# A graph network on one core: the last five layers multiply by whole float32 features and widened counts

## The reference, cut to what matters

```python
for l in range(5):
    agg = segment_sum(h[src], dst, 6250)
    x = (h + agg) @ W1[l] + b1[l]
    x = relu(bn(x, bn1_g[l], bn1_b[l]))
    x = x @ W2[l] + b2[l]
    x = relu(bn(x, bn2_g[l], bn2_b[l]))
    h = relu(bn(x, bn3_g[l], bn3_b[l]))
```

## Time and profile before

| | us |
|---|---|
| median of the timed runs | 11149.94 |
| lowest and highest timed run | 11141.5, 11180.91 |
| span of the profiled execution | 11182.9 |
| TensorE matmuls busy in the span | 6422.3 (57%) |
| VectorE, ScalarE, GpSimd busy | 4061.9, 3980.1, 4429.3 |

### The profile page before, as it was taken

How to read it: one execution, slowest core, us unless ns; L and a number is a source line. 1 busy time by engine, 2 the same in 40 slices (tenths; PEclk the granted TensorE clock), 3 DMA queues, 4 the chain that set the end, 5 groups by cost and what they waited for, 6 DMA issues and landing times. The chain is left out here.

```text
span 11182.9 us, 142834 instructions
## 1 busy us (share of the span) xinstructions
PE 6422.3 (57%) x34150; PEld 4429.5 (40%) x34151; DVE 4061.9 (36%) x11422; ACT 3980.1 (36%) x8307; POOL 4429.3 (40%) x4465
## 2 busy tenths in 40 slices
PE   1611112642367787355554555545554989898997
PEld 1600001630012575255553555535554444444443
DVE  3800001442278787444444444534445020201112
ACT  2046662002278775344443444434444010101001
POOL 3866667247710000366664666466664000000000
PEclk8555555765578898677776777777777999999998
DMA  4332223534433442133332333233332546464554
GB/s 122 95 88 86 87 85 111 144 104 121 123 120 117 142 133 88 45 72 72 72 71 64 71 72 72 58 76 71 71 72 49 181 146 200 141 202 140 167 173 134
DMA packets 1106637, 1190.87 MB, mean 106 GB/s; under 512 B 118423, under 2 KB 991526, under 8 KB 1105944
## 3 DMA queue, kind: packets, MB, share of 16 engines
q1 hardware_dynamic: 710164, 628.94, 19.0%
q0 software_dynamic: 150784, 336.22, 12.6%
q10 hardware_dynamic: 245444, 222.71, 7.1%
HBM read 973.07 MB, written 216.86 MB: 106 GB/s over the span
## 5 line engine op out<-in xcount | busy, mean ns | idle before, releaser
L1196 POOL DMA_INDIRECT ring<-gat_rows,src_idx x2496 | 2426.2, 972 | 1550.8 <-issue 946.1
L1316 PE MATMUL ps<-ring,xT_b 128*128 x8192 | 1494.4, 339 | 1697.0 <-ACT xT_b L1402 1091.5
L1316 PEld LDWEIGHTS ps<-ring,xT_b 128*128 128x128 f32 x8192 | 1312.4, 243 | 1884.8 <-issue 1883.4
L1394 ACT ACTIVATE xT_a<-xT_a,state 128x514 f32<-128x514 f32 x1024 | 742.6, 725 | 2370.7 <-DVE xT_a L1364 1751.7
L1364 DVE CUSTOM_DVE_ANT_0 xT_a<-ps,mask,xT_a 128x512 f32<-128x512 f32 x1024 | 768.9, 751 | 2241.7 <-remote 1361.7
L1622 PE MATMUL ps<-xT_b,features 128*128 128x504 f16 (+1 forms) x5655 | 1198.3, 367 | 0.0
L690 POOL DMA_INDIRECT by_src<-ring,state x832 | 806.7, 970 | 462.1 <-issue 462.1
L1307 PE MATMUL ps<-ident,s_col 128*128 128x128 f32 x4096 | 750.3, 316 | 214.0 <-issue 129.9
L1622 PE MATMUL ps<-adj_tile,features 128*128 128x504 f16 (+1 forms) x3900 | 827.4, 367 | 0.0
L1046 POOL TENSOR_TENSOR x_nodes<-x_nodes,state 128x1280 f32<-128x1280 f32 x12 | 39.4, 3311 | 1971.2 <-DMA ring<-gathered 1254.2
L1817 POOL TENSOR_TENSOR features<-xT_a,features 128x640 bf16<-128x640 f32 x40 | 56.1, 1402 | 1919.7 <-DVE features L1814 1919.7
(11 more groups left out here) (379 smaller groups left out, 8639.2 us busy)
## 6 DMA issues: line engine op xcount, KB each, us to landing
dl_all<-dloc_rows ACTq DMA_DIRECT2D x1052, 128.0 KB
xT_b<-adjacency SPq DMA_DIRECT2D x145, 882.0 KB, 4.8
xT_b<-adjacency SPq DMA_DIRECT2D x145, 756.0 KB, 4.6
adj_tile<-adjacency SPq DMA_DIRECT2D x100, 882.0 KB
adjacency<-xT_b ACTq DMA_DIRECT2D x319, 252.0 KB
adj_tile<-adjacency SPq DMA_DIRECT2D x100, 756.0 KB
ring<-by_src SPq DMA_DIRECT2D x52, 1040.0 KB
ring<-gathered SPq DMA_DIRECT2D x208, 260.0 KB
```

Of the source, the lines that this page charges most:

```text
L1196: pool.indirect_dma_start(ring[:, o:o + RC], None, table[:, :], bass.IndirectOffsetOnAxis(src_idx[:, t * W + u:t * W + u + 1], 0)).then_in ...
L1316: m = pe.matmul(bank(BO + v % 2, R), pw[v % 4][:, w * P:(w + 1) * P], ring[:, w * RC:][:, bass.ds(look(SLOT, u - 7), R)], start=w == 0, st ...
L1394: act.activation(um[u % 4], sm[u % 8], ACT.Identity, bias=S[:, ER:][:, bass.ds(look(BC, u), 1)]).then_inc(q["act_a"], 1)
```

## The change

It is in four parts.

1. The features stay whole float32 (`H`, 128 columns a block), and so do the sums of the extra runs (`V`), `run_hit` and the extra counts (`extra_of`, laid out anew). There is one matmul a window in place of three, with float32 on both sides. The split is gone: `feature_to_node` and a load of the first two tiles (`preload`) take its place between layers, three copies (ScalarE, VectorE, GpSimd) and the same load before the first layer.
2. Since the counts are multiplied in float32, `widen(n)` makes a float32 copy of each 16-bit tile: VectorE the first 4 windows and ScalarE the other 3 (in part two 3 and 3, the last one narrow), into one of two buffers. TensorE waits for both halves (`eq`, `eq2`) instead of for the load; the two engines wait for the load, and for TensorE to be through with the tile two before. SyncE reloads a tile's buffer when it has been widened.
3. The taking out of part one and its bias and statistics stand inside the loop over part two, in the order of the engines' programs between the widenings.
4. The count matrix lies in DRAM in rows of 6552 counts (`adj`: 49 x 128 x 6552). A tile's load is one run of 7056 bytes a partition instead of seven of 1008. ScalarE's loop over the 319 pairs is written out; a pair that straddles two source blocks is stored with two DMAs (24 such). To make room the buffers of the earlier stages are given back before, with one more copy (`kept_extra`) and one more barrier.

```diff
-        adj = dram("adjacency", (2 * PAIRS, P, WD), F16)
+        adj = dram("adjacency", (NB, P, NWIN * WD), F16)
...
+            def widen(n):
+                k, i = divmod(n, NB)
+                b, f = n % NT, n % 2
+                for eng in (dve, act):
+                    if n >= KEPT:
+                        eng.wait_ge(q[f"ld{b}"], 16 * (n // NT + (b >= KEPT)))
+                    if n >= 2:
+                        eng.wait_ge(q["product"], n - 1)
+                cut, end = cuts[k]
+                dve.tensor_copy(wide[f][0][:, 0:cut], tiles[b][:, 0:cut]).then_inc(q["eq"], 1)
+                act.activation(wide[f][1][:, 0:end - cut], tiles[b][:, cut:end], ACT.Copy).then_inc(q["eq2"], 1)
...
             for k, ws in enumerate(parts):
                 for i in range(NB):
                     b = n % NT
                     if n >= NT:
-                        sp.wait_ge(q["product"], n - NT + 1)
+                        sp.wait_ge(q["eq"], n - NT + 1)
+                        sp.wait_ge(q["eq2"], n - NT + 1)
                     if n >= KEPT:
                         load_tile(i, ws, b)
-                        pe.wait_ge(q[f"ld{b}"], 16 * (n // NT + (b >= KEPT)))
-                    for x in range(3):
-                        h = H3[:, (i * 3 + x) * D:(i * 3 + x + 1) * D]
...
+                    if n == NB + 1:
+                        evict(parts[0])
+                    widen(n)
+                    if n == 1:
+                        dve.wait_ge(q["bcast"], 1)
+                        s(dve, lambda: dve.tensor_copy(V[0:NV, :], of_runs))
+                    if k and i % 5 == 1 and (i - 2) // 5 - 2 in parts[0]:
+                        bias_and_stats((i - 2) // 5 - 2)
+                    pe.wait_ge(q["eq"], n + 1)
+                    pe.wait_ge(q["eq2"], n + 1)
+                    h = H[:, i * D:(i + 1) * D]
+                    for j, w in enumerate(ws):
+                        v = wide[n % 2][0][:, j * WD:j * WD + width] if o < 0 else wide[n % 2][1][:, o:o + width]
+                        m = pe.matmul(bank(w % 8, width), h, v, start=i == 0, stop=False)
+                        if lo < hi:
+                            pe.matmul(bank(w % 8)[:, lo - w * WD:hi - w * WD], h, ident[:, lo - i * P:hi - i * P],
+                                      start=False, stop=False)
...
+        cuts = [(4 * WD, 7 * WD), (3 * WD, 5 * WD + width_of(NWIN - 1))]
+        wide = [(nsb(f"wide{f}", 4 * WD), nsb(f"wide{f + 2}", 3 * WD)) for f in range(2)]
...
-            sp.dma_start(tiles[b][:, 0:len(ws) * WD].rearrange("p (w c) -> p w c", c=WD),
-                         adj[i * NWIN + ws[0]:i * NWIN + ws[-1] + 1, :, :].rearrange("w p c -> p w c")
-                         ).then_inc(q[f"ld{b}"], 16)
+            n = cuts[ws[0] // DW][1]
+            sp.dma_start(tiles[b][:, 0:n], adj[i, :, ws[0] * WD:ws[0] * WD + n]).then_inc(q[f"ld{b}"], 16)
...
         with nc.Fori(0, GIN - 1) as l:
             layer(l)
-            split_features(False)
+            preload()
+            feature_to_node(XTb, H, D, ACT.Relu, aff[:, 0:1], aff[:, 1:2])
```

More of the change, by code:

```diff
@@ L145, in build @@
         Wst = sb("w_static", 8 * D)
-        Wext = sb("w_ext", 4 * (D + 2))
         vec = sb("vectors", 128)
@@ L1551, in evict @@
                     act.activation(banks[u], out4[u], ACT.Copy, scale=0.0).then_inc(q["evac"], 1)
-                    if u or not first:
+                    if u or it:
                         store(it * 4 + u - 1, (u - 1) % 4)
[L1555 to L1558, removed]
             store(PAIRS - 1, (PAIRS - 1) % 4)
             for u in range(4):
-                act.wait_ge(q[f"st{u}"], 16 * (PAIRS // 4 + (u < PAIRS % 4)))
+                act.wait_ge(q[f"st{u}"], stored[u])
             end_phase(gather_first_layer(TABLES, T))
@@ L1584, in first_weights, with evict @@
                           ).then_inc(q["mm"], 1)
-            by_block = extra[:, :].rearrange("p (c b) -> p b c", b=NBP)
+            def evict(ws):
+                for w in ws:
+                    if w % 2 == 0:
+                        dve.wait_ge(q["summed"], w + 1)
+                        dve.tensor_copy(window(w), bank(w % 8, width_of(w))).then_inc(q["evac"], 1)
+                    else:
+                        act.wait_ge(q["summed"], w + 1)
+                        act.activation(window(w), bank(w % 8, width_of(w)), ACT.Copy).then_inc(q["out"], 1)
@@ L1594, in neighbours @@
[L1594 to L1603, removed]
@@ L1759, in build, with nsb @@
         layer_norm()
+        kept_extra = XTa[:, 0:NV * NBP].bitcast(F32)
+        dve.tensor_copy(kept_extra.rearrange("p (b c) -> p c b", c=NV), extra[:, :].rearrange("p (c b) -> p c b", b=NBP)
+                        ).then_inc(q["chain"], 1)
+        end_phase()
         gat_only.close()
[L1763 to L1766 removed]
+        gin_only = ctx.enter_context(ExitStack())
+        def nsb(name, cols, dt=F32):
+            return gin_only.enter_context(nc.sbuf_tensor(name, [P, cols], dt))
+        H = nsb("features", NBP * D)
+        V = nsb("extra_sums", D)
+        run_hit = nsb("run_hit", NB * P)
+        extra_of = nsb("extra_wide", NV * NBP)
+        parts = [range(0, DW), range(DW, NWIN)]
+        width_of = lambda w: min(WD, NB * P - w * WD)
+        cuts = [(4 * WD, 7 * WD), (3 * WD, 5 * WD + width_of(NWIN - 1))]
+        wide = [(nsb(f"wide{f}", 4 * WD), nsb(f"wide{f + 2}", 3 * WD)) for f in range(2)]
+        tiles = [nsb(f"adj_tile{i}", DW * WD, F16) for i in range(2)] + \
             [XTb[:, i * DW * WD // 2:(i + 1) * DW * WD // 2].bitcast(F16) for i in range(NT - 2)]
```

149 lines of the change are left out of this document (59 added, 90 removed).

## The result

The changed kernel takes 11752.42 us, the median of 4 runs (11675.7 to 11769.0). The kernel before takes 11162.35 us beside it (4 runs, the three above and one more, 11141.5 to 11180.91). The ratio is 1.0521, 95% interval 1.0475 to 1.0568. The interval puts it between 11680 and 11783 us. So the kernel is slower, by the mechanism forecast, but by clearly less than forecast; the measured value lies outside the range, though the low end of the range lies inside the interval.

What follows compares the result with a forecast made beforehand. The prediction took TensorE as the only bound in the five layers; 678 + 19 + 5 - 35 - 16 + 8 = +659 us on a median of 11150 gave 11809 us, range 11750 to 11920, chance 0.85.

Steps and rivals of the forecast that it cites:

- the price of the product: Five layers' matmuls: float32 windows at 0.847 us against 0.637 for three 16-bit matmuls; +135.5 us a layer, +678 in five.
- a narrow matmul: The 61 float32 matmuls of 128 columns a layer: taken at 0.25 us each, bounds 0.215 and 0.37.
- D: Rival in the product: float32 passes overlap more than separate matmuls, making the kernel faster, 10.79 ms; chance 0.03.
- the large form of A: Rival in the product: float32 weight loads come into the open, 637 us more, 12.4 ms; chance 0.07 with the small form.
- the widening is hidden: VectorE's and ScalarE's float32 copies of each tile, at most 2.7 and 1.5 us, run beside TensorE's matmuls; costed at nothing.
- A's small form: Rival: a hand-over of 0.2 us a tile between widening and TensorE, +98 us, 11.91 ms; chance 0.07 with the large form.
- B: Rival in the layers: VectorE's widening becomes the bound at 7.5 us a tile of part one, 12.4 ms; chance 0.03.
- C: Rival in the product: TensorE's granted clock falls to 0.50, adding 2.7 ms, to 14.5 ms; chance 0.02.
- Layer start, end and turn: Around each layer's product: start +3.8 us a layer (+19), end +1 (+5), four turns between layers -8.7 each (-35).
- Set-up: Before the first layer: -16 us for the first split's removal, +8 for added copies, barrier and float32 `run_hit`.
- Making the counts: Count stage, ScalarE's loop written out and 24 more stores: taken at 0, bounds -10 and +20 us.
- the spread of the runs: Part of the forecast's own range, for the whole kernel's timed runs: -8 to +31 us.

Runs made afterwards that it cites:

- e7_two_pieces: The kernel before without the third bfloat16 piece of the features in the product: 10689.12 us, ratio 0.9408.
- e4_narrow_widen: The changed kernel, but from a layer's third tile on VectorE and ScalarE widen only 8 counts each: 11947.34 us, ratio 1.0520.
- e2_unrolled: The kernel before with only ScalarE's loop over the 319 pairs written out, the count matrix laid out as before: 11305.05 us, ratio 0.9979.
- e3_order: The kernel before with ten buffers of the earlier stages placed in memory where the changed kernel has them: 11328.94 us, ratio 1.0003.

## Why the prediction was right and where it was wrong

**Right: TensorE bounds the layers, and the price of the product.** Forecast 543.7 us a layer, measured 541.43, so +133.3 a layer in place of +135.5: +666 of the forecast +678. A window is 0.846 us, not 0.847, and a narrow matmul 0.22, at the low bound. That leaves no room for D, which needed 0.64 us a window or less, nor for the large form of A; `e7_two_pieces` shows that the passes of one float32 matmul take as long as separate 16-bit matmuls do. A page of the Trainium skill bears on it: "FP8 and Floating Point Precision", section "TensorE Precision Notes", has true float32 as four passes through the array, and 275.8, 408.2 and 541.4 us for two, three and float32 agree.

**Right: the widening is hidden** (1.21 and 1.47 us, under the bounds of 2.7 and 1.5), shown by `e4_narrow_widen`. A's small form, the hand-over, and B don't occur, and neither does C, with the product's clock at 1.00.

**Layer start, end and turn.** Start: forecast +3.8 a layer, measured +2.7 in the first and +2.0 in the second (13.6 and 13.0 against 10.9). In the first layer the clock was 0.50 in the first six us, as taken, and 13.5 matmuls (27 records) went through in them, where 14 were taken; but a short matmul was 6.00 / 28 = 0.21 us at 0.99, not 0.25. In the second layer the clock was 0.72 there. End, from the product to the last step of the statistics: +1 forecast, 13.2 against 12.0 us measured. Turn: -8.7 forecast, 14.66 against 23.08 measured, -8.4. By these, 666 + 11 + 6 - 34 = 649, and the landmark gives 648.4.

**Set-up: -8 forecast, -13.3 measured.** The 7.6 us of loads and barrier were taken at 10, and the copies of 2600 counts took 2.86 and 1.52 us, not up to 3.5 each. That is at the low end of its bounds.

**The step that failed: "Making the counts ... Bounds -10 and +20; I take 0, since the 2 us of ScalarE arithmetic a pair are unchanged."** The arithmetic is indeed unchanged, 1.98 us. But the stage's pace was not the arithmetic alone: of the 300 us in the earlier trace rows ScalarE idles 34, and the sum has no term for what that idle time is. For the most part it is a pause of 0.87 us at each lap of the hardware loop: 34 laps in those 300 us, and 59 laps, 51 us, from the end of the gathers to the end of the stage. Written out, the stage takes 27 to 34 us less (`e2_unrolled` 1254.5 against `e3_order` 1282.6; after 1183.0 against 1217.3), outside the lower bound of -10. After the gathers 0.108 us are won on each pair of windows, and there are 237 of them in the kernel before on the first chip and 268 in `e3_order`: 26 to 29 us; that is about half of the pause, and the other half goes to waits that the view puts down to TensorE. While GpSimd gathers, a pair takes several times as long (74 and 78 pairs in the first 670 us on the first chip, 42 to 45 on the others in all but one run, which has 51), and the loop shows no steady effect there. The Trainium skill speaks for the gain: "Runtime: NRT & Kernel Launch", section "Instruction fetch mechanics", says that a taken branch whose target lies outside the stretch of instructions at hand has to wait for them, and that this is one reason why kernels prefer to be unrolled. The pause at each lap goes the same way, but no run shows whether the start of this short lap lies outside that stretch. The register load alone does not make the pause: `e2_unrolled` still has one before every fourth pair, and of these pairs 17 of 67 come late, against 12 to 15 of 67 at the other three places. Whether it is instruction fetch, the branch itself or the computed addresses, no run here separates.

With -29 for this step in place of 0, -12 for the product, -6 for start, end and turn together, and -5 for the set-up, the forecast becomes 11757 us. The ratio on the other chip, 1.0546, gives 11759 on the median of before. Both are still inside the range, 7 and 9 us above its low end. The 26 us from 11757 to 11731 lie inside the interval of the first ratio (1.0475 to 1.0568 is 104 us wide here), and in the profiled pair the early stages, which the change doesn't touch, are 28 us shorter. So the counts are the largest wrong term, far outside its own bounds, and with the smaller ones they use up 52 of the 59 us between the forecast and the low end; that the measured value then fell outside the range is the spread of the runs, which the range had taken at -8 to +31 us from three runs of before. That part is bad luck and a term taken too narrow, not a mechanism.

**What stays open:** what makes the pause at the lap, and what sets the pace of the count stage once the loop is gone (a wait put down to TensorE, mostly at every seventh pair).

## What to carry to other kernels

Whole float32 matmuls cost as much as four 16-bit passes here. Where the other operand is exact in 16 bits, as small whole numbers are, three bfloat16 pieces beat them, and two float16 pieces, with 22 bits at most, beat both. Price each operand format in passes before asking whether its conversion can be hidden. Where an edit writes out a hardware loop on an engine near its bound, look in the timeline for a pause at the lap's period, and don't trust the releaser that is named beside it. The pause times the laps that run at the engine's own pace is the upper bound of the gain; here half of it came, and the other half went to waits put down to TensorE.

## What the runs showed of the hardware beyond this

Chips of one kind differ by 1.6% in this kernel (11149.94 against 11328 us), but not where TensorE sets the pace: the layers take 2456.5 us on the first and 2456.2 on the other. The difference lies mostly where GpSimd gathers rows: the making of the counts (1217.3 and 1282.6) and the stages up to the last matmul of attention (4899.0 and 4970.4). GpSimd's own gathers, first in the kernel before, then in `e3_order`:

```profile
L1196 POOL DMA_INDIRECT ring<-gat_rows,src_idx x2496 | 2426.2, 972 | 1550.8 <-issue 946.1 <-SPq L1172 604.7
```

```profile
L1196 POOL DMA_INDIRECT ring<-gat_rows,src_idx x2496 | 2409.4, 965 | 1642.5 <-issue 945.5 <-SPq L1172 696.9
```

The gathers are issued as fast (972 and 965 ns), but GpSimd waits 92 us longer for room in the ring (L1172). What makes the ring slower to come free on the other chip, no run shows. So the time of a whole program is compared only with a time of the same chip, and a stage's landmark says which part of a difference is the chip's.
